# A two-layer graph network on one Trainium2 core: 34 tiles' sums scaled beside layer 0's last batches, late x1 rows stored behind h1's, nine h1 tiles among the heads

## The reference, cut to what matters

```python
# x: 6250 x 512, 100000 edges (src, dst)
h = relu(layernorm(x))
# layer 0: graph attention, 8 heads of 64
feat = h @ W[h];  logit = leaky_relu(alpha_s[src] + alpha_d[dst])
att  = softmax of logit over the edges of one src
x1   = x + relu(segment_sum(att * feat[dst], src))        # "agg"
h1   = relu(layernorm(x1))
# layer 1: on h1
agg  = segment_mean(batchnorm(h1)[src], dst);  conv = relu(agg @ W_conv + b_conv)
attn = linear attention with random features on the first 256 rows of h1 (8 heads), @ Wo
out  = x1 + batchnorm(conv + attn + h1)
```

## Time and profile before

| what | us |
|---|---|
| median of three runs | 2991.46 |
| the profiled execution's own time | 2990.22 |
| its span | 2988.3 |
| PE, DVE, POOL, ACT busy | 2506.1, 2172.9, 1834.8, 994.0 |
| layer 0's last add (DVE) ends | 1557.3 |
| first and last start of layer 1's gathers | 1706.9, 2696.5 |

### The profile page before, as it was taken

One profiled execution on the slowest core, in us unless ns is written; L12 is line 12 of the kernel. 1 busy time (PEld: TensorE's weight loads), 2 busy tenths in 40 slices (PEclk: granted clock), 3 DMA queues, 4 the chain that ended last, 5 costly groups with the idle time before them and its releaser, 6 DMA issues. The chain is left out here.

```text
span 2988.3 us, 45996 instructions
## 1 busy us (share of the span) xinstructions
PE 2506.1 (84%) x10647; PEld 1547.5 (52%) x10692; DVE 2172.9 (73%) x3788; ACT 994.0 (33%) x3078; POOL 1834.8 (61%) x1881
## 2 busy tenths in 40 slices
PE   5887728999999999999978888888888889999990
PEld 4555416777777777777767733333333333334440
DVE  8999988898889888988988655444444444445668
ACT  6843335555555555555543600000000000002220
POOL 0000036777777777777747167777777777774658
PEclk8998859999999999999998999999999999999995
DMA  6110047888888888888755887777777777773218
GB/s 207 52 40 37 37 140 221 241 242 246 246 240 244 245 245 238 246 246 244 240 188 157 285 286 210 210 210 209 210 210 210 210 210 209 210 210 127 67 56 294
DMA packets 243451, 588.26 MB, mean 197 GB/s; under 512 B 57745, under 2 KB 82833, under 8 KB 243401
## 3 DMA queue, kind: packets, MB, share of 16 engines
q0 software_dynamic: 133120, 443.52, 50.6%
q1 hardware_dynamic: 110280, 144.14, 14.7%
HBM read 533.43 MB, written 54.10 MB: 197 GB/s over the span
## 5 line engine op out<-in xcount | busy, mean ns | idle before, releaser
L517 POOL DMA_INDIRECT big<-feat_table,idx x880 | 837.4, 952 | 685.8 <-ACT idx L542 407.8
L1141 POOL DMA_INDIRECT big<-h_table,idx x784 | 741.9, 946 | 309.0 <-issue 218.2
L812 PE MATMUL psA<-big,onehot 128*128 128x260 f32 x1760 | 440.1, 393 | 16.0 <-DVE big L694 13.9
L812 PE MATMUL psB<-big,onehot 128*128 128x260 f32 x1760 | 433.4, 389 | 7.3
L568 ACT ACTIVATE big<-big,late_weights 128x65 f32<-128x65 f32 x1760 | 434.1, 340 | 0.0
L812 PEld LDWEIGHTS psA<-big,onehot 128*128 128x128 f32 x1760 | 317.8, 190 | 101.0 <-issue 37.0
L812 PEld LDWEIGHTS psB<-big,onehot 128*128 128x128 f32 x1760 | 316.9, 190 | 64.2 <-DVE acc L704 17.6
L542 ACT CAST idx<-minorB 128x8 int32 (+1 forms) x101 | 20.2, 203 | 946.2 <-DMA big<-h_table,idx 946.2
L1570 DVE TENSOR_TENSOR acc<-acc,psCD 128x512 f32 x176 | 120.7, 686 | 206.9 <-PE psCD L1879 204.8
L1570 DVE TENSOR_TENSOR acc<-acc,psA 128x512 f32 x176 | 120.7, 686 | 206.6 <-PE psA L1879 204.0
L1878 PE MATMUL psCD<-big,onehot 128*128 x352 | 185.2, 608 | 47.9 <-ACTq L1294 41.9
(11 more groups left out here) (446 smaller groups left out, 3829.1 us busy)
## 6 DMA issues: line engine op xcount, KB each, us to landing
nodes_all<-slot_nodes SPq DMA_DIRECT2D x56, 512.0 KB, 5.9
big<-feat_table,idx POOLq DMA_INDIRECT x880, 3.8
feat_table<-big SPq DMA_DIRECT2D x49, 264.0 KB, 2.1
h_table<-big SPq DMA_DIRECT2D x49, 256.0 KB, 3.5
x_table<-acc SPq DMA_DIRECT2D x49, 256.0 KB, 9.1
big<-h_table,idx POOLq DMA_INDIRECT x784, 3.7
big<-h_table SPq DMA_DIRECT2D x49, 256.0 KB, 2.6
big<-x_table SPq DMA_DIRECT2D x49, 256.0 KB, 4.7
```

Source lines behind the costliest of these rows:

```text
L517: g.indirect_dma_start(ring[:, b.k, q * SB + u, :], None, feat_table, bass.IndirectOffsetOnAxis(ap=idx[:, 2 * b.k + q, u:u + 1], axis=0)). ...
L812: ins = pet.matmul(psum[:, 512 * hf:512 * hf + HALF_W], onehot[:, q, u % SB, :], ring[:, b.k, u, HALF_W * hf:HALF_W * (hf + 1)], start=(u ...
L1141: g.indirect_dma_start(big[:, place:place + D], None, h1_table, bass.IndirectOffsetOnAxis(ap=idx[:, r.c % CHUNK_CYCLE, b:b + 1], axis=0)). ...
```

## The change

Four things. (1) Tiles 0 to 33 (EARLY = 34) get their reciprocals in the pass of batch 53 and are scaled by POOL right behind its last gather; the other 15 follow when all lots are added. `xlast` is cleared within the last batch, and two passes leave the DVE's loop to be written out. (2) x rows are loaded after the second lot of the last batch, and DVE runs x1 slots 0 to 3 ahead of the "first_tiles" steps. (3) x1 rows 0 to 19 are stored in their own slots, ahead of the refill of `xin`; rows 20 to 48 after `grams` is 49. (4) h1 tiles 40 to 48 are made by ACT two by two at the start of heads 0 to 4, and their grams stand at the end of PE's work for the same heads.

```diff
-        X1_BESIDE_H1 = 32
+        X1_EARLY = 20
+        EARLY, EARLY_LOTS = 34, LB * (BATCHES - 2)
+        assert (E + EARLY * (LOT - 1)) // LOT <= EARLY_LOTS
+        def heads_tiles(h):
+            return range(min(TILES, 40 + 2 * h), min(TILES, 42 + 2 * h))
...
-            sp.wait_ge(lot_added, ADD_CREDIT + ROWS * LOTS)
+            sp.wait_ge(lot_added, ADD_CREDIT + (ROWS - 2) * LOTS + 2)
             for q in range(4):
                 sp.dma_start(xin[:, q, :], x[q * P:(q + 1) * P, :]).then_inc(x_in[q], 16)
...
+            sp.wait_ge(lot_added, ADD_CREDIT + ROWS * LOTS)
             for u in range(2):
                 sp.dma_start(proj_s[:, :, u, :], proj.rearrange("(t p) d -> p t d", p=P)).then_inc(proj_loaded, 16)
             for t in range(TILES):
                 sp.wait_ge(x1_ready, t + 1)
+                if t < X1_EARLY:
+                    store_x1(t)
                 if t + 4 < TILES - 1:
                     sp.dma_start(xin[:, t % 4, :], x[(t + 4) * P:(t + 5) * P, :]).then_inc(x_in[t % 4], 16)
                 for u in range(TILES):
                     if h1_store_slot(u) == t:
                         store_h1(u)
-                        if u >= X1_BESIDE_H1:
-                            store_x1(u - X1_BESIDE_H1)
...
-            pool.wait_ge(lot_ps, RING_CREDIT + LB * (BATCHES - 1))
-            PG.done(g.iota(path_numbers, ...), "iota")
-            pool.wait_ge(den_ready, 1)
-            with pool.Fori(0, TILES) as t:
+            pool.wait_ge(den_ready, 1)
+            with pool.Fori(0, EARLY) as t:
+                scale_sums(t)
+            pool.wait_ge(lot_ps, RING_CREDIT + LB * (BATCHES - 1))
+            PG.done(g.iota(path_numbers, ...), "iota")
+            pool.wait_ge(den_ready, 2)
+            with pool.Fori(EARLY, TILES) as t:
                 scale_sums(t)
...
+            def reciprocal_sums(first, end):
+                den = maxd[:, first:end, :]
+                link(v.tensor_scalar(den, head_cols[:, first:end, :, O], 1e-30, None, ALU.max))
+                v.reciprocal(den, den).then_inc(den_ready, 1)
...
                     if nxt and a == 1:
                         make_onehotT(aft, 0)
+                        if nxt.i is None and nxt.c == BATCHES - 1:
+                            dve.wait_ge(lot_added, ADD_CREDIT + EARLY_LOTS)
+                            reciprocal_sums(0, EARLY)
+                    if last and a == LB - 3:
+                        v.memset(xlast, 0.0).then_inc(zeroed, 1)
...
-            with dve.Fori(0, BATCHES // 2) as i:
+            with dve.Fori(0, BATCHES // 2 - 1) as i:
                 for c in range(2):
                     pass_batch(Batch(i, c), Batch(i, c + 1))
+            for n in range(BATCHES - 3, BATCHES - 1):
+                pass_batch(batch(n), batch(n + 1))
             pass_batch(batch(BATCHES - 1), None)
 
             dve.wait_ge(lot_added, ADD_CREDIT + ROWS * LOTS)
-            v.memset(xlast, 0.0).then_inc(zeroed, 1)
-            link(v.tensor_scalar(maxd[:, :, :], head_cols[:, :, :, O], 1e-30, None, ALU.max))
-            v.reciprocal(maxd[:, :, :], maxd[:, :, :]).then_inc(den_ready, 1)
+            reciprocal_sums(EARLY, TILES)
...
-            for t in range(TILES - X1_BESIDE_H1, TILES):
+            for t in range(X1_EARLY, TILES):
                 store_x1(t)
...
-            for t in range(40, TILES):
-                h1_tile(t)
             for h in hs:
+                for t in heads_tiles(h):
+                    h1_tile(t)
                 SPE.wait(act, f"qfT{h}")
...
+            x1_upto(4)
             dve.wait_ge(sortB_done, 2)
...
-            for t in range(40, TILES):
-                gram(t)
...
                 if h < H - 1:
                     turn_q(h + 1)
+                for t in heads_tiles(h):
+                    gram(t)
```

More of the change, by code:

```diff
@@ L525, in layer0_gpsimd @@
             gather_batch(batch(BATCHES - 1))
-            pool.wait_ge(lot_ps, RING_CREDIT + LB * (BATCHES - 1))
-            PG.done(g.iota(path_numbers, [[1, PATH]], base=0, channel_multiplier=0, allow_small_or_imprecise_dtypes=True), "iota")
-            pool.wait_ge(den_ready, 1)
             def scale_sums(t):
@@ L534, in scale_sums @@
                                 .broadcast_to([P, H, O]), ALU.mult).then_inc(x_scaled, 1)
-            with pool.Fori(0, TILES) as t:
+            pool.wait_ge(den_ready, 1)
+            with pool.Fori(0, EARLY) as t:
+                scale_sums(t)
+            pool.wait_ge(lot_ps, RING_CREDIT + LB * (BATCHES - 1))
+            PG.done(g.iota(path_numbers, [[1, PATH]], base=0, channel_multiplier=0, allow_small_or_imprecise_dtypes=True), "iota")
+            pool.wait_ge(den_ready, 2)
+            with pool.Fori(EARLY, TILES) as t:
                 scale_sums(t)
@@ L705, in add_lot @@
                                 ALU.add).then_inc(lot_added, 1)
+            def reciprocal_sums(first, end):
+                den = maxd[:, first:end, :]
+                link(v.tensor_scalar(den, head_cols[:, first:end, :, O], 1e-30, None, ALU.max))
+                v.reciprocal(den, den).then_inc(den_ready, 1)
             def pass_batch(this, nxt):
                 aft = nxt.ahead(1) if nxt else None
+                last = not nxt
                 if this:
```

## The result

The changed kernel takes 2996.73 us (median of 20 runs, 2990.91 to 3000.60), the kernel before beside it 2989.84 (20 runs, 2982.54 to 2994.46). The ratio is 1.0021 with an interval of 1.0015 to 1.0027: **slower by some 6 us**, where the forecast had 3.5 us faster. Each boundary is an event of the timeline.

What follows compares the result with a forecast made beforehand. The prediction had the end hang on layer 1's 25th gather, its first freed places bound by SP. Terms 5.4 + 0 - 5.0 + 2.2 - 6.1 gave -3.5 us, 2991.5 to 2988.0; the 8-in-10 range was 2979 to 2996.

Steps and rivals of the forecast that it cites:

- A: Layer 0's last hand-over, DVE beside POOL's scaling: 25th gather +5.4 us, between +1.4 and +15.8, with 4.0 of waits.
- the list of fourteen: The 14 DVE operations of the hand-over that don't read PSUM and may wait for POOL; upper bound 14.4 us.
- The rule I weighed there: Trainium skill: DVE instructions with two SBUF inputs contend with POOL instructions reading SBUF; hand-over waits at their upper bound.
- B: Layer 0's last add to PE's transposes: shift 0, between -1 and +2 us; PE waits for the new order.
- C: Features of k, DVE without POOL beside it: -5.0 us, between -2.3 and -7.0.
- The step on the clock: Features of k: DVE earlier, PE's 2.29 us wait goes; 14.7 us at low clock shrink by up to 7 us.
- D: Last grams put among layer 1's first heads: first gather +2.2 us, between +1.5 and +3.5.
- E: SP's x1 stores and the ring, first to 25th gather: -6.1 us, between -3.2 and -9.5.
- no x1 stores stand before them to fill the queue: SP's 29 stores behind the grams: three slow ones fewer save 4.0 us, three more going quickly 2.1.
- the port taken in full: Rival: POOL back to back holds each of the 14 hand-over operations, 15.8 there; +8.9 us, 3000.4, chance 0.15.
- The gather comes no sooner: Rival: transfers bound SP's stores and the clock falls all the same; +2.1 us, 2993.6, chance 0.17.
- the signs named ahead: Forecast wrong if layer 0's last add moves under 3 or over 9 us, the end hangs elsewhere, or x rows delay DVE.

Runs made afterwards that it cites:

- experiment 1: Kernel before with only the early reciprocals, 34 early scalings and written-out passes; 2999.54 us against 2992.35, ratio 1.0025.
- Experiment 3: Changed kernel with x1 slots 0 to 3 put behind the first_tiles steps again; 2999.11 us against 2992.35 for the kernel before, ratio 1.0021.
- experiment 2: Changed kernel without early scaling, all 49 tiles scaled behind the last add; 2994.36 us against 2992.35 for the kernel before, ratio 1.0007.
- experiment 9: Kernel before with the norm2_g and norm2_b loads moved behind SP's loop that frees the ring; 2993.07 us against 2994.98, ratio 0.9993.
- experiment 10: Kernel before with norm2 loads moved, grams among the heads, late x1 rows mostly stored among the last h1 rows; 2992.58 us against 2994.98, ratio 0.9992.
- experiment 8: Kernel before with the last nine grams among the heads and x1 rows 0 to 19 stored early, no early scaling; 2989.98 us against 2990.58, ratio 1.0000.
- experiment 11: Kernel of experiment 10 with 14 tiles scaled early, behind the hand-over; 2990.44 us against 2994.98 for the kernel before, ratio 0.9985.
- experiment 4: Changed kernel with POOL's first 34 scalings held until batch 54's first weighing is done; 3008.67 us against 2992.35 for the kernel before, ratio 1.0053.
- 6: Kernel of experiment 4 with its late maximum written with two SBUF inputs; 3008.07 us against 2990.58 for the kernel before, ratio 1.0055.
- 7: Kernel of experiment 4 with a fill and an addition put on DVE ahead of the late maximum; 3010.03 us in one run.

## Why the prediction was wrong

**A failed, and it decides.** The step was "eight separate waits of half an instruction, 4.0". Ten instructions waited 0.76 each, three more 0.04 to 0.28: 8.2 us of waits. The mechanism and the list of fourteen were right (thirteen of them were longer), and rows in hand pointed to the size: 1.00 for 0.17 in the earlier trace rows is a wait of 0.83. The ten waits are nearly alike, 0.66 to 0.89, so that these dependent instructions met POOL at about the same phase each time. I set that row aside for a mean over all phases. The rule I weighed there would have given the upper bound, 14.4; the measured 8.2 lies between that and my 4.0, and beyond the 7.5 from which I had said that the change loses. Left out of A was PE: I had it hiding some of DVE's waits, when in fact its own idle times grew to 3.99 and 3.78 us, and the stretch behind the second, at the lower clock, took 1.5 more (0.3 and 0.4 in the kernels of 1 and 3). That the earlier trace rows priced just such a fall in C should have put it into A. The early reciprocals took 0.9 for the 1.4 of the forecast.

**B was right in sum**, 15.1 as forecast. Experiment 3 shows that the order, to which the forecast gave the 4.1 us gained ahead of x1, is worth 1.4 us at the transposes and nothing later; with the tables first, x1 starts 4.2 us behind the last add (5.6 in the kernel before), and the transposes follow it at the old distance of 9.5.

**C was right in sum** (-4.1 for -5.0), and half of its reason held. That DVE gains when POOL is out of its way is borne out: the early scaling alone (experiment 1) moved C by -4.9, and from the last add to the last sum_kv the changed kernel takes 5.6 us less than that of experiment 2. The step on the clock failed. It took the wait of 2.29 and the low stretch in the earlier trace rows for a price that goes only if DVE gets faster, and experiment 9 has neither with DVE's program unchanged, and a longer low stretch ahead of the features in their place. There the whole of C is 114.5, so the swap of one low stretch for the other gains nothing that counts; that the sum came out near is in part luck.

**D was right** (+2.6 for +2.2; the grams ended 21.2 us behind, 21.5 to 21.7 forecast).

**E failed in size**: the step "no x1 stores stand before them to fill the queue", 14 slow ones instead of 20. The 29 rows took 32.2 us, three rows fewer gave 2.0. That rows stored early leave the same rate behind them says that the pace there doesn't come from a filled queue; experiments 9 and 10 show what does hold the 25th gather, SP's own list, the 2.9 us of norm2_b in it. D and E together are +0.7, not -3.9, and experiment 8 has them at +0.7 in its trace and at nothing in its ratio.

**The rivals and the range.** The rival that came nearest by its shift is the port taken in full, at 0.15: +8.9 forecast, with 15.8 for A against 10.8 measured. "The gather comes no sooner" has -5.5 for C and E together, near the measured -6.0, and A at 5.4: its +2.1 and the 5.4 that A lacked are +7.5, and the stages A to E add up to +7.4. I treated port, stores and clock as alternatives, though they were independent and two misses in one direction were enough: 4 us of stores and 5 of the port. The range ended at 2996.0, below 2996.73. The terms' bounds as stated add up to -14.6 and +15.8, not to -15 and +19. Of the signs named ahead, one came: the last add moved by more than 9 us.

## What to carry to other kernels

Before work goes onto POOL beside a DVE chain, list the chain's instructions with two SBUF inputs and charge each, by what was measured here, about three quarters of a POOL instruction (0.76 of 1.03 us). Beside instructions that read PSUM the same work did no harm, in an amount that ended soon behind them (experiment 11); with more of it, 18 us were lost behind them (experiment 4). A wait that is gone at the consumer is worth only what the producer's own start doesn't lose, so read the first transfer and the one that waited together, as in experiment 10. And where an engine that feeds TensorE gets slower, price TensorE's clock behind the idle time too.

## What the hardware showed that I had not expected

- A DVE instruction with all its inputs in SBUF can be shut out far longer than one POOL instruction: 18.92, 18.5 and 18.25 us in three kernels (4, 6, 7), each time to the end of 34 back-to-back scalings, while a fill of 0.16 passed just ahead of it (7). In the changed kernel's hand-over, beside the same loop of 34, no wait was over 0.9 us. What tells the two apart wasn't found.
- One-input instructions wait as well: a TENSOR_SCALAR on 8 partitions took 1.11 instead of 0.27, a cast of four elements 1.04 instead of 0.15. A maximum over 280 elements beside POOL took 0.27 in experiment 11.
- An idle time of TensorE of only 3.8 us was followed by 6 us at a granted clock of 0.50 to 0.59, near the level of 1.2 GHz, and then 1.00 again; idle times of 3.75 us in two other kernels (1, 3) were followed by some 3 us at 0.51 to 0.55.
- Two executions of the same instructions, in the kernel before and in that of 9, had their low clock at different places between the transposes and the last sum_kv, and still took 114.95 and 114.5 us in all.
